# Attention layer of a graph network: the gathered rows scaled eight tiles at a time, straight from the PSUM bank in which their weights were turned

## The reference

```python
Wh = einsum('ni,hio->hno', x, W)                       # 4 heads x 32 features of each node
e  = leaky_relu(e_l[:, src] + e_r[:, dst], 0.2) + log(clip(edge_weight, 1e-8))
alpha = exp(e.T - segment_max(e.T, dst)[dst])          # one weight for each edge and head
msgs  = alpha / (segment_sum(alpha, dst)[dst] + 1e-8) * Wh[src]
out   = segment_sum(msgs, dst) + bias
x = x + out
```

## Time and profile before

| what | us |
|---|---|
| median of 3 runs | 7595.03 (7585.03 to 7601.97) |
| the profiled execution's own time | 7576.51 |
| its span, first to last instruction | 7574.6 |
| PE busy | 5788.0 (76% of the span) |
| DVE busy | 3964.2 (52%) |
| ACT busy | 2413.6 (32%) |
| POOL busy | 1950.0 (26%) |
| granted clock of TensorE, mean | 0.882 of full speed |

### The profile page before, as it was taken

One profiled execution on the slowest core, in us unless ns is written; L12 is line 12 of the kernel. 1 busy time (PEld: TensorE's weight loads), 2 busy tenths in 40 slices (PEclk: granted clock), 3 DMA queues, 4 the chain that ended last, 5 costly groups with the idle time before them and its releaser, 6 DMA issues.

```text
span 7574.6 us, 166058 instructions
## 1 busy us (share of the span) xinstructions
PE 5788.0 (76%) x48472; PEld 4914.5 (65%) x48472; DVE 3964.2 (52%) x10698; ACT 2413.6 (32%) x7276; POOL 1950.0 (26%) x1782
## 2 busy tenths in 40 slices
PE   1777777777777779999999999997255666556665
PEld 1555555555555569999999999997134444444444
DVE  6999999999999972221111111112244444444444
ACT  2666666666666641111110000002021222222222
POOL 2000000000000000000000000002777777777771
PEclk9998899899999989999999999997677777777776
DMA  6676676666766776676666666662122222222221
GB/s 205 280 284 278 274 287 278 279 278 278 287 275 276 286 296 270 260 277 260 277 277 277 277 277 277 277 277 77 48 58 56 56 56 57 58 56 56 56 57 32
DMA packets 261013, 1542.61 MB, mean 204 GB/s; under 512 B 56235, under 2 KB 86965, under 8 KB 233836
## 3 DMA queue, kind: packets, MB, share of 16 engines
q1 hardware_dynamic: 201380, 1406.77, 47.2%
q0 software_dynamic: 59008, 129.85, 6.4%
q10 hardware_dynamic: 130, 0.80, 0.0%
HBM read 795.75 MB, written 743.08 MB: 203 GB/s over the span
## 4 chain that ended last, share of the span: by engine, by line
PE 45%; DVE 18%; POOL 15%; issue 13%; ACT 3%; ACTq 3%; DMA 2%; DVEq 0%; SPq 0%; POOLq 0%
PE psum L1118 29%; POOL field L810 15%; DVE field L1549 12%; PE psum L1083 7%; PE psum L1307 2%; PE psum L1285 2%; ACT field L923 2%; ACTq L908 2%; DVE field L1542 1%; ACT field L1014 1%; DVE field L1543 1%; DVE field L1544 1%; ACTq L923 1%; DMA field<-adj 1%; PE psum L1184 1%
## 5 line engine op out<-in xcount | busy, mean ns | idle before, releaser
L1118 PE MATMUL psum<-field 128*128 128x128 f32 x19208 | 2256.0, 277 | 21.1 <-issue 19.3
L1118 PEld LDWEIGHTS psum<-field 128*128 128x128 f32 x19208 | 2233.1, 189 | 21.8 <-issue 19.7
L1083 PE MATMUL psum<-field 128*128 128x200 bf16 (+1 forms) x14112 | 1918.5, 280 | 134.3 <-DVE field L1549 117.9
L923 ACT COPY field<-psum x4704 | 1658.6, 416 | 953.9 <-PE psum L1083 662.6
L810 POOL DMA_INDIRECT field<-head_table,cmp x1563 | 1621.2, 1037 | 476.4 <-issue 468.7
L1549 DVE TENSOR_TENSOR field<-field 128x1176 bf16<-128x1176 bf16 x2352 | 1647.9, 759 | 0.0
L1083 PEld LDWEIGHTS psum<-field 128*128 128x128 bf16 x14112 | 1074.8, 101 | 426.8 <-issue 160.6
L1074 PE MATMUL psum<-zero_b 128*128 128x2 bf16 x4704 | 806.6, 171 | 455.9 <-ACT field L923 450.7
L1074 PEld LDWEIGHTS psum<-zero_b 128*128 128x128 bf16 x4704 | 477.1, 101 | 642.2 <-issue 578.6
L754 POOL DMA_INDIRECT field<-tile_rows,step_t_i x74 | 200.6, 2710 | 2398.4 <-PE psum L1054 2351.9
L1014 ACT COPY field<-psum x1611 | 433.6, 269 | 1037.8 <-PE psum L1307 725.7
(11 more groups left out here) (289 smaller groups left out, 2690.2 us busy)
## 6 DMA issues: line engine op xcount, KB each, us to landing
adj<-field SPq DMA_DIRECT2D x882, 800.0 KB, 5.1
field<-adj SPq DMA_DIRECT2D x196, 3200.0 KB, 10.0
field<-head_table,cmp POOLq DMA_INDIRECT x1563
field<-in_edge_attr SPq DMA_DIRECT2D x4, 3072.0 KB, 23.5
head_table<-field SPq DMA_DIRECT2D x7, 476.0 KB, 3.2
tile_rows<-field SPq DMA_DIRECT2D x1, 3328.0 KB, 18.0
right_edges<-zeros SPq DMA_DIRECT2D x1, 3328.0 KB, 19.8
place_rows<-right_edges SPq DMA_DIRECT2D x25, 128.0 KB, 2.8
```

The source lines that it names most:

```text
L923: act.copy(evac[:, :, bass.ds(place, SEG)], build_banks[:, bass.ds(bank, NSEG * SEG)].rearrange("p (w c) -> p w c", w=NSEG)).then_inc(pair ...
L1083: mm = pe.matmul(build_banks[:, bass.ds(cur[j % ROUND], end - first)], hot, pr[:, first:end], start=False, stop=True, skip_group_check=True)
L1118: mm = pe.matmul(ps_y[slot][:, 0:D], source[:, hi, :], adj_in[slot][:, :, 2 * hi:2 * hi + 2], start=(hi == 0), stop=(hi == NB - 1))
```

## The change

The rows of a group are scaled by one `tensor_tensor` over up to eight tiles in place of one `scalar_tensor_tensor` for each tile. Its second operand is not the copy in SBUF but the bank `ps_alpha` itself, walked as tile, head, and the same weight 33 times. ACT's copy L994, its buffer `alpha` and its semaphore `alphas_copied` are gone; DVE waits for PE's `alphas_turned` in its place. Each product is the same fp32 product of row and weight.

```diff
@@ ScalarE, weights()
                 act.wait_ge(exponents_ready, w + 1)
                 act.activation(score[0:n, :, :], score[0:n, :, :], ACT.Exp).then_inc(alphas_ready, 1)
-                act.wait_ge(alphas_turned, w + 1)
-                act.copy(alpha[:, :, 0:n], ps_alpha[:, 0:HEADS3 * WIN].rearrange("p (h t) -> p h t", h=HEADS3)[:, :, 0:n])\
-                    .then_inc(alphas_copied, 1)
@@ VectorE, the end of softmax()
                 dve.sem_inc(exponents_ready, 1)
-                dve.wait_ge(alphas_copied, w + 1)
+                dve.wait_ge(alphas_turned, w + 1)
@@ VectorE, steps_of()
                     if t < tiles:
-                        for u in range(t, min(t + SUB, tiles)):
-                            r = rows[:, i * WIN + u, :, 0:DH3 + 1]
-                            al = alpha[:, :, u].rearrange("p (h a) -> p h a", a=1).to_broadcast([P, HEADS3, DH3 + 1])
-                            ins = dve.scalar_tensor_tensor(out=r, in0=r, scalar=1.0, in1=al, op0=ALU.mult, op1=ALU.mult)
-                        ins.then_inc(rows_scaled, 1)
+                        n = min(SUB, tiles - t)
+                        r = rows[:, i * WIN + t:i * WIN + t + n, :, 0:DH3 + 1]
+                        al = ps_alpha[:, 0:HEADS3 * WIN].rearrange("p (h t) -> p h t", h=HEADS3)[:, :, t:t + n]\
+                            .rearrange("p h t -> p t h").rearrange("p t (h a) -> p t h a", a=1).to_broadcast([P, n, HEADS3, DH3 + 1])
+                        dve.tensor_tensor(r, r, al, ALU.mult).then_inc(rows_scaled, 1)
```

More of the change, by code:

```diff
@@ L265, in build @@
         right_e, score, fwd, bwd = (a.rearrange("p (h e) -> p h e", h=HEADS3) for a in (right_f, score_f, fwd_f, bwd_f))
-        alpha = piece(HEADS3 * WIN).rearrange("p (h t) -> p h t", h=HEADS3)
         win_logw = piece(DEPTH * P)[0:WIN, :].rearrange("p (i e) -> p i e", i=DEPTH)
@@ L418, in build @@
         alphas_turned = sem("alphas_turned")
-        alphas_copied = sem("alphas_copied")
         rows_scaled = sem("rows_scaled")
```

## The result

| | before | after |
|---|---|---|
| median, us | 7597.1 (7585.0 to 7602.0, 4 runs) | 7471.65 (7467.1 to 7475.4, 4 runs) |
| ratio | | 0.9837, 95% interval 0.982 to 0.9854 |
| span of the profiled execution, us | 7574.6 | 7469.4 |
| windows 1 to 23, us | 1980.6 | 1866.9 |
| gathers above 1.35 us in them | 128 | 0 |

The account below looks back on a forecast made before the run. The prediction took POOL's gathers, some held by DVE's scalings, to bound the kernel. 115.7 us of stalls plus 1.8 us at the windows' start made 117.5 us: 7595.0 to 7477.5 us, range 7450 to 7500.

Parts of the forecast that it names:

- POOL's pace sets windows 1 to 23: Windows 1 to 23: 86.1 us each, paced by POOL's gathers; the rest of the machine has 11.7 us to spare.
- All stalls above 1.35 us go, 115.7 us: Gathers of windows 1 to 23: 128 long ones, held by L1898's second SBUF operand, lose 115.7 us of excess.
- The prediction's own argument: L1834, one PSUM operand, held none of 24 gathers; L1800, both in SBUF, stretched POOL's DMA from 0.98 to 1.81 us.
- the trace agrees on both: Skill page's rule: two SBUF inputs on VectorE contend with GpSimd's SBUF reads, at most one does not; trace said to agree.
- The small excesses stay, as they lie on L1903: Gathers of windows 1 to 23: the other 15 us of excess stays, as L1903 is unchanged.
- The scaling takes 1.26 us, worth nothing inside a window: New DVE scaling: 1.26 us against 1.74 for eight of L1898; no gain mid-window, where DVE waits for PE.
- 0.9 us for the window's start, twice, 1.8 us: Turned weights to first product: 0.40 us without ACT's copy plus 0.48 from the first scaling, counting in windows 23 and 24.
- The sign that the prediction gave for this term: End of the stage: the time from the last gather to the end would be 2 us shorter.
- The median moves as the sum says: Whole kernel: 117.5 us off the profiled execution and off the median alike, 7595.0 to 7477.5 us.
- The rival of stalls that stay: New scaling: any long DVE access to `rows` stops gathers, 5.0 us a window as now; 7593 us, chance 4%.
- the slower one: New scaling: slow PSUM read of about 2.4 us that also holds POOL; 211 us slower, 7806 us, chance 2%.
- PE as the bound: Windows of gathers: DVE and PE need more than 81.1 us, so the gain stops there; 7535 us, chance 4%.

Follow-up runs that it names:

- single tiles: Changed kernel with eight scalar_tensor_tensor a group in place of its one instruction, weights still from PSUM, no ACT copy: 7472.1 us, ratio 0.9847.
- added work out of PSUM: Changed kernel with three more tensor_tensor after each scaling, one operand in PSUM, results unused: 7474.1 us, ratio 0.9855.
- the batched run: Kernel before with one tensor_tensor for eight tiles, weights still from ACT's copy in SBUF: 7588.8 us, ratio 1.0003.
- the added work: Changed kernel with three more tensor_tensor after each scaling, both operands in SBUF, results unused: 7528.5 us, ratio 0.9928 (third run).
- the scalings with waits: Kernel before with a semaphore wait between the eight scalings, weights in SBUF: 9135 and 9140 us, ratios 1.0186 and 1.0153, both on slow chips.

## Why the prediction was right, point by point

- *POOL's pace sets windows 1 to 23.* Right. The stretch shortened by exactly what the gathers did, 113.7 us, and 244 us of added DVE work did not lengthen it.
- *All stalls above 1.35 us go, 115.7 us, since the second operand leaves SBUF.* Right: none is left in the profile above, and one each in those of the single tiles and of the added work out of PSUM (1.43 us at most); a second profile of the changed kernel had three, 1.46 us at most, with 1.4 us of excess in all. These five lie on the softmax, on instructions of 64 partitions with both operands in SBUF. The longest of them, in the second profile of the changed kernel (DVE, then POOL), ends 0.83 us after L1830:

```profile
6968.60 0.68 DVE L1830 SCALAR_TENSOR_TENSOR work<-work 64x512 f32<-64x512 f32 x1
```
```profile
6968.65 1.46 POOL L808 DMA_INDIRECT field<-head_table,cmp  x1 [0.30 <-issue]
```

The runs that separate operand, count, opcode and place all say the operand. The prediction's own argument for it had a gap: in the trace of before 19 gathers came to their critical point in L1836, a tensor_tensor with both operands in SBUF, and none was held. They came within 0.085 us of its start, and that is too early to be held, as the last section tells. Of the 24 beside L1834 two came in its first 0.16 us and prove nothing; 19 came over 0.18 us into it. The sentence of the Trainium skill ("SBUF — State Buffer", "Who interferes with whom") that tensor_tensor does not stall the making of descriptors is contradicted, for these indirect DMAs, by the batched run and by the added work: 73 and 70 gathers held for more than 0.4 us. The prediction left out a condition of the rule on one SBUF input, which on that page holds outside the 2-port performance modes only, and "the trace agrees on both" is too strong: L1903 has one SBUF input, and 96 of the 227 gathers that met it in windows 1 to 23 of before had over 0.04 us of excess.
- *The small excesses stay, as they lie on L1903.* The sum is right, 15.4 us before and 16.5 after, but in part by luck. Only 7.8 of the 15.4 us lay on L1903 (8.1 after); 4.7 lay on the scalings, which kept 0.8, and those on the softmax rose from 2.9 to 7.7 us. In the other profiles with the weights in PSUM and the one-hot instructions unchanged, the work added out of PSUM included, the sum was 13.6 to 14.4 us.
- *The scaling takes 1.26 us, worth nothing inside a window.* 1.245 us, by the group of 195 full ones.
- *0.9 us for the window's start, twice, 1.8 us.* Mis-sized in what reached the end. The path is shorter by 0.9 us in window 23 (first turned scores to first product 16.8 us against 17.7), but from there to window 24's first turn took 55.85 us against 55.19, and from the last window's first gather to the end 177.8 against 178.2. PE's first products alone take 3.50 us after at a granted clock of 0.54, 3.23 us before at 0.59. 0.4 us arrived, and in the six other profiles from the usual chips that stretch was 177.8 to 186.4. The sign that the prediction gave for this term, 2 us less from the last gather to the end, did not come: 142.2 us before, 144.1 after, as the last window's gathers too were done sooner (33.7 us in place of 36.0).
- *The median moves as the sum says.* 125.4 against 117.5; the two profiled executions differ by 105.2 only. The stage began at 5335.1 us before and at 5344.0 after, though nothing ahead of it changed, and between 5337.7 and 5343.0 in the other profiles of the usual chips. This scatter of some 9 us lies outside the change; 113.7 + 0.4 - 8.9 = 105.2. So the traces account for 114.1 us of gain, near the 115.1 us between the medians on the later chip; the 11 us beyond it in the 125.4 are not accounted for.

The rival of stalls that stay was refuted by the gathers, the slower one by the scaling's 1.245 us, and PE as the bound by its remaining wait of 7.4 us a window. That another chip would have another bound stood in no rival.

## What to carry to other kernels

When GpSimd issues indirect DMAs back to back and sets the pace, compare their median with their mean and look at which VectorE instruction each long one ends behind. Take the second operand of that instruction from PSUM, if it is there anyway, or put a pause between such instructions (this took the stalls away, its gain in time was not measured on a usual chip); merging them into one doesn't help by itself. Before trusting a gain of a per cent, see whether other chips have the same bound.

## What the runs showed of the hardware that was not expected

- A gather is held to the end of a whole run of VectorE instructions with two SBUF operands (up to 1.58 us of excess over eight), unless DVE pauses between them: then 0.125 us at most. A gather caught in the last 0.03 us of the one-hot instructions before such a run is held as well (28 in the batched run out of SBUF).
- A gather has one sensitive point, 0.13 us after its start; 0.82 to 0.85 us after the release it is done.
- An instruction that follows a pause doesn't hold a gather at once. In the eight profiles from the usual chips 77 gathers came to their point in the first 0.15 us of the softmax's second addition (L1836 before, L1831 after, 64x512, both operands in SBUF), and the largest excess was 0.012 us; the seven that came later were all held to its end, the longest for 0.48 us. This fits the scalings with waits: 0.295 us long, they held for 0.125 us at most.
- The running-maximum scans on 64 partitions, which also have two SBUF operands, seldom held a gather: of 143 met in the kernel before, one had more than 0.04 us of excess. That is a matter of when the gathers came. Of 561 met by the forward ones (L1846 before) in the eight profiles, 287 came in the first 0.18 us of a scan, 14 of them with over 0.04 us of excess, and 257 after 0.3 us, 0.039 us at most. The 17 in between were all held, for 0.13 to 0.18 us.
- Of the five chips of the later runs, two ran the kernel before at 8976 and 9002 us in place of some 7585; the other runs on them show ACT's waits as told above.
